# A DLRM tower with three interaction layers: embedding lookups spread otherwise, dense features turned earlier, tile 0 loaded whole, tile 1 loaded from ScalarE's queue

## The chip, the cores and the metric

One core of one Trainium2 chip. The metric is the device time in microseconds (us). Engines: TensorE (PE), VectorE (DVE), ScalarE (ACT), GpSimd (POOL), and SyncE (SP), which in this kernel only issues DMAs.

## The reference, cut to what matters

```
e = stack of 32 table rows per sample                    # 1024 x 32 fields x 16 values, fp32, tables of 1000 to 125000 rows
x0 = h = e                                               # B, F=32, E=16
for W, b in 3 layers:                                    # a compressed interaction network
    z = (x0[:, :, None, :] * h[:, None, :, :])           # B, F*G, E: all products of a field of x0 and a row of h
    y = relu(einsum('oc,bce->boe', W, z) + b)            # 128 rows out
    keep, h = y[:, :64], y[:, 64:]   (last layer: both y)
z = sum over E of all kept rows                          # B x 256
h = concat([z, dense_ctx])                               # B x 272
y = relu(relu(h @ W_top1 + b1) @ W_top2 + b2) @ W_top3   # 512, 256, 1
```

## The kernel before, in words

**Tiles.** The 1024 samples are eight blocks of 128, and a block is four tiles: a tile is four of the 16 embedding values of 128 samples, so it has 512 columns. There are 32 tiles. In the trace a tile takes some 29 to 31 us once the kernel is under way.

**A slot.** The engines work through slots, one per tile. Slot n holds layer 0 of tile n+1, layer 1 of tile n and layer 2 of tile n-1, in an order written out by hand (`SLOT`). An item `(layer, n)` is two chunks of 128 products: VectorE multiplies (`multiply`, L1069), TensorE multiplies the products by the weights (L616). Layer 2 is computed in three passes over split numbers: VectorE writes the product (`unsplit`), ScalarE rounds it (`high`, L828), GpSimd takes the difference (`low`, L499), and TensorE multiplies high by two weights (L624) and then low by one (L639). The last pass of an item stands behind the next item's passes in TensorE's order, and TensorE waits there if GpSimd is not done. Seven of layer 2's eight items go through GpSimd, (2,0) to (2,5) and (2,7); (2,6) is not split. The ring of these buffers has four entries.

**GpSimd's order.** It also issues the lookups: 32 indirect DMAs for each block (`look_up`, L489), one per field, eight per slot, for the block after the current one. Which item they stand behind is a table, `LOOKUPS_AFTER`, with one row for the slot in which a new block's indices are taken (quarter 0) and one for the other three; `LOOKUPS_FIRST` is the number ahead of the first item. In quarter 0 the indices are copied to `ids_now` (L476) by `begin`, behind item (2,2) and the tail (L507), after all lookups of the block before have landed.

**What a tile needs from HBM.** TensorE turns the tile's rows (`turn_x`, L588), ScalarE copies them to `xrows` (`take_x`, L808), SyncE stores them to HBM (`xcols`, L393, 96 KB) and reads them back, once the store has landed, in three layouts: `shifted` (L400, four DMAs of 256 KB) for layer 0, `shifted_tail` (L405, four of 64 KB), and `spread` (L415, four of 1 MB, one per group g of four chunks) for layers 1 and 2. All of them are issued by SyncE in one program order and go to one queue (q1 in the page). The fourth group of a tile is loaded in the next tile's round. Tile 0's `shifted` is not loaded but made by transposes (L671, `FIRST_ORDER`).

**The prologue.** SyncE loads the weights; VectorE and ScalarE reorder them; TensorE turns them in ten groups (`turn`, L560; groups 0 and 1 are layer 0's, 2 to 5 layer 1's, 6 to 9 layer 2's) into two PSUM banks in turn, and VectorE copies each out (L1002; for layer 2 L996, L997 and L1000), so group n waits for the copy of group n-2. Behind all ten TensorE turns the dense features (L576), ScalarE copies them (L784, L786), and VectorE takes their low parts (L1013, L1015). ScalarE's next instruction is the copy of block 0's looked-up rows (`take_rows`, L792), on which GpSimd's `begin` for block 1 and tile 0 depend. GpSimd issues block 0's 32 lookups at once from the start, and behind `begin(1)` another 8 at once; the last three quarters of block 1 follow in the first three slots.

## Time and profile before

| | us |
|---|---|
| median of 3 runs (lowest, highest) | 1094.03 (1093.96, 1094.55) |
| the profiled execution's own time | 1094.61 |
| its span, first to last instruction | 1092.8 |
| PE busy | 1004.2 (92%) |
| DVE busy | 820.0 (75%) |
| POOL busy | 820.0 (75%) |
| ACT busy | 473.9 (43%) |
| DMA, mean of 16 engines | 170 GB/s |

The page's strip of 40 slices has PE at 9 tenths in nearly every slice behind the third, and lower at three places: the first three slices (82 us), slice 13 and slice 29. The granted clock is 8 or 5 tenths in the first slices and drops by a tenth in the same two places later. The rows of timelines further down read: start in us from the span's start, duration in us, engine, line, operation, output<-inputs, shape, count, and in brackets how long the engine was idle before it and what ended that wait.

### The profile page before, as it was taken

To read this page: it belongs to the slowest core of one execution; us is meant where nothing else is said; L and a number is where in the kernel's file an instruction comes from. 1 tells how busy PE (TensorE), PEld (TensorE's weight loads), DVE (VectorE), ACT (ScalarE), POOL (GpSimd) and SP (SyncE) were. 2 spreads that over 40 slices of the span, in tenths; PEclk is the share of its full clock that TensorE was granted. 3 is DMA by queue.
4 is the path that set the end of the run, shared out by engine and by line. 5 is a ranking of instruction groups with operands and counts; after the bars stand their busy time and mean duration, and the time that the engine had idled before them with its cause. 6 is when DMAs were issued, how large, how long until landed. Compare 5 with 4: busy or idle time off the path is not lost.

```text
span 1092.8 us, 11324 instructions
## 1 busy us (share of the span) xinstructions
PE 1004.2 (92%) x3089; PEld 573.0 (52%) x3089; DVE 820.0 (75%) x750; ACT 473.9 (43%) x595; POOL 820.0 (75%) x524
## 2 busy tenths in 40 slices
PE   2168999999989999999999999999899999999988
PEld 2133555555545555555555555555455555555555
DVE  4245787888774887888778877988578877888882
ACT  2132444444443454444535544444335444454453
POOL 6555779797969879797988889797788866666650
PEclk8588999999998999999999999999899999999999
DMA  7079988799985889799987988899787988889200
GB/s 154 5 167 205 208 198 181 166 206 206 193 185 119 187 192 204 158 195 203 201 182 161 201 197 184 171 200 206 155 182 163 198 200 189 189 197 205 75 1 0
DMA packets 49012, 185.45 MB, mean 170 GB/s; under 512 B 17570, under 2 KB 22178, under 8 KB 28388
## 3 DMA queue, kind: packets, MB, share of 16 engines
q1 hardware_dynamic: 40804, 183.15, 75.9%
q0 software_dynamic: 8192, 2.11, 2.1%
q8 instruction: 7, 0.11, 0.1%
q14 instruction: 9, 0.07, 0.0%
HBM read 182.06 MB, written 3.15 MB: 169 GB/s over the span
## 4 chain that ended last, share of the span: by engine, by line
PE 41%; POOL 24%; issue 18%; DVE 8%; ACT 4%; another core or an unknown queue 3%; DMA 2%; SPq 1%; DVEq 0%; POOLq 0%; ACTq 0%
PE y L616 25%; POOL low L499 13%; POOL looked_up L489 9%; PE y L624 9%; PE y L639 5%; DVE unsplit L1069 2%; DVE prod L1069 2%; DVE acc_kept L1100 1%; POOL tail_parts L507 1%; DMA spread<-in_L_rec_W 1%; ACT h L814 1%; PE xT L588 1%; DMA xcols<-xrows 1%; DMA shifted<-xcols 1%
## 5 line engine op out<-in xcount | busy, mean ns | idle before, releaser
L499 POOL TENSOR_TENSOR low<-unsplit,high 128x1024 fp32r<-128x1024 f32 x221 | 530.7, 2411 | 137.3 <-ACT high L828 133.3
L616 PE MATMUL y<-prod,w1T 128*128 128x512 f32 x1024 | 479.3, 596 | 6.1 <-DVE prod L1069 3.3
L1069 DVE TENSOR_TENSOR prod<-spread,h 128x1024 f32<-128x1024 f32 x288 | 346.5, 1213 | 86.5 <-PE y L616 73.5
L828 ACT CAST high<-unsplit 128x1024 fp32r<-128x1024 f32 x224 | 234.1, 1045 | 324.4 <-DVE unsplit L1069 312.8
L1069 DVE TENSOR_TENSOR unsplit<-spread,h 128x1024 f32<-128x1024 f32 x224 | 271.5, 1213 | 102.3 <-ACT h L814 83.8
L489 POOL DMA_INDIRECT looked_up<-in_tbl,ids_now x256 | 246.8, 964 | 75.7 <-issue 71.9
L616 PEld LDWEIGHTS y<-prod,w1T 128*128 128x128 f32 x1024 | 193.1, 191 | 168.0 <-issue 148.4
L624 PE MATMUL y<-high,w2T_high 128*128 128x512 f32 x448 | 227.6, 508 | 1.4 <-ACT high L828 1.4
L639 PE MATMUL y<-low,w2T_high 128*128 128x512 f32 x448 | 203.9, 536 | 22.4 <-POOL low L499 22.1
L624 PE MATMUL y<-high,w2T_low 128*128 128x512 f32 x448 | 178.1, 397 | 0.0
L814 ACT ACTIVATE h<-y,bias 64x512 f32<-64x512 f32 x128 | 83.3, 651 | 165.2 <-PE y L616 156.5
L639 PEld LDWEIGHTS y<-low,w2T_high 128*128 128x128 f32 x448 | 83.1, 191 | 113.0 <-issue 62.7
L616 PE MATMUL y<-prod,w0T 128*128 128x512 f32 x256 | 123.7, 606 | 7.5 <-DVE prod L1069 7.5
L624 PEld LDWEIGHTS y<-high,w2T_high 128*128 128x128 f32 x448 | 85.3, 190 | 47.6 <-issue 28.3
L624 PEld LDWEIGHTS y<-high,w2T_low 128*128 128x128 f32 x448 | 85.1, 190 | 44.0 <-issue 29.5
L1069 DVE TENSOR_TENSOR prod<-shifted,xT 128x1024 f32<-128x1024 f32 x64 | 77.6, 1212 | 25.7 <-DMA shifted<-xcols 20.2
L616 PEld LDWEIGHTS y<-prod,w0T 128*128 128x128 f32 x256 | 49.1, 193 | 51.8 <-issue 47.7
L616 PE MATMUL y<-prod,w2T_whole 128*128 128x512 f32 x128 | 61.9, 607 | 0.0
L1100 DVE TENSOR_TENSOR acc_kept<-acc_kept,kept 128x512 f32<-128x512 f32 x24 | 54.8, 2282 | 0.0
L507 POOL TENSOR_TENSOR tail_parts<-tail,tail_high 128x512 fp32r<-128x512 f32 x32 | 41.0, 1280 | 15.1 <-ACT tail_high L852 15.0
L820 ACT ACTIVATE kept<-y,bias_kept 64x512 f32<-64x512 f32 x64 | 43.7, 682 | 1.6
L808 ACT COPY xrows<-xT 48x512 f32<-48x512 f32 x32 | 18.5, 578 | 44.4 <-PE xT L588 33.2
(115 smaller groups left out, 409.5 us busy)
## 6 DMA issues: line engine op xcount, KB each, us to landing
spread<-xcols SPq DMA_DIRECT2D x128, 1024.0 KB, 9.0
shifted<-xcols SPq DMA_DIRECT2D x124, 256.0 KB
shifted_tail<-xcols SPq DMA_DIRECT2D x124, 64.0 KB
looked_up<-in_tbl,ids_now POOLq DMA_INDIRECT x256
xcols<-xrows SPq DMA_DIRECT2D x32, 96.0 KB
spread<-in_L_rec_W SPq DMA_DIRECT2D x3, 512.0 KB, 6.7
spread<-in_L_rec_W SPq DMA_DIRECT2D x1, 1024.0 KB
wt<-in_W_top SPq DMA_DIRECT2D x2, 512.0 KB, 9.9
```

The costliest lines, as they stand in the source:

```text
L489: pool.indirect_dma_start(out=looked_up[:, f, :], out_offset=None, in_=tables[f][:, :], in_offset=bass.IndirectOffsetOnAxis(ap=ids_now[:, ...
L499: pool.tensor_tensor(low[kind][r][:, :, :], unsplit[kind][r][:, :, :], high[kind][r][:, :, :].bitcast(F32), ALU.subtract).then_inc(s_low[k ...
L507: pool.tensor_tensor(tail_parts[:, :], tail[:, :], tail_high[:, :].bitcast(F32), ALU.subtract).then_inc(s_tail_low, 1)
L616: last = pe.matmul(y[:, :], w, z[:, c, :], start=(n == 0 and c == 0), stop=(item in (LAST0, LAST1) and c == ITEM - 1))
L624: pe.matmul(y[:, :], w[:, ITEM * n + c, :], z[:, c, :], start=(n == 0 and c == 0 and w is w2T_high), stop=False)
L639: last = pe.matmul(accumulator(s, layer)[:, :], w2T_high[:, ITEM * n + c, :], z[:, c, :], start=False, stop=(item == LAST2 and c == ITEM - 1))
L808: act.copy(xrows[:, :], xT[0:XROWS, :]).then_inc(s_xrows, 1)
L814: last = act.activation(h[to, :], y[lanes, :], ACT.Relu, bias=bias[lanes, :])
L820: act.activation(kept[t[1] % 2][lanes, :], y[lanes, :], ACT.Relu, bias=bias_kept[lanes, :]).then_inc(s_kept, 1)
L828: act.copy(high[kind][r][:, :, :], unsplit[kind][r][:, :, :]).then_inc(s_high[kind], 1)
L1069: dve.tensor_tensor(z, x[:, ITEM * n:ITEM * (n + 1), :], b[:, :].unsqueeze(1).to_broadcast([P, ITEM, COLS]), ALU.mult).then_inc(s_made[kin ...
L1100: dve.tensor_tensor(acc_kept[:, :], acc_kept[:, :], z[:, :], ALU.add).then_inc(s_sum_kept, 1)
```

## The change

Four edits. (1) Another table of lookups: in quarter 0 two stand behind (2,2), that is right behind `begin`, none behind (2,3), one behind (2,4), two behind (2,5), three behind (2,7); in the other quarters one ahead of the first item, and one, one, one, two, two behind (2,2), (2,3), (2,4), (2,5), (2,7). (2) TensorE turns the dense features behind layer 1's weights, ahead of layer 2's, and VectorE takes their low parts ahead of its copies of layer 2's weights. (3) Tile 0's four `spread` groups are loaded one after the other. (4) Tile 1's store, its four `shifted` and its four `shifted_tail` loads are issued by ScalarE, right behind its copy of tile 1's rows, with a wait of ScalarE for the store's landing; SyncE waits for the same landing before it issues tile 1's first three `spread` groups.

```diff
--- before.py
+++ after.py
@@ -91,8 +91,8 @@
 
 ADD_KEPT_AFTER = (2, 1)
 FOLD_KEPT_AFTER = (2, 2)
-LOOKUPS_AFTER = ((0, 0, 0, 2, 2, 2, 2), (0, 0, 1, 2, 1, 1, 1))
-LOOKUPS_FIRST = (0, 2)
+LOOKUPS_AFTER = ((0, 0, 2, 0, 1, 2, 3), (0, 0, 1, 1, 1, 2, 2))
+LOOKUPS_FIRST = (0, 1)
 
 
 def kind_of(item, last):
@@ -386,16 +386,13 @@
                            (bias_last[:, :], b2)):
                 sp.dma_start(to, of.rearrange("(p a) -> p a", a=1)).then_inc(s_biases, 16)
 
-            def load_shifted(t):
-
-
+            def store_x(t):
                 sp.wait_ge(s_xrows, number(t) + 1)
                 sp.dma_start(xcols[number(t)], xrows[:, :]).then_inc(s_xcols, 16)
                 sp.wait_ge(s_xcols, 16 * (number(t) + 1))
+
+            def load_shifted(t):
                 x = xcols[number(t)]
-                if isinstance(t[0], int) and number(t) == 0:
-
-                    return
                 for j in range(GROUP):
                     sp.dma_start(shifted[FIELDS * j:FIELDS * (j + 1), :, :],
                                  bass.AP(x.tensor, x.offset + GROUP * j * COLS,
@@ -418,10 +415,9 @@
                              ).then_inc(s_spread[k % 2][g], 16)
 
             def load_factors(t):
+                store_x(t)
                 load_shifted(t)
-
-                if not isinstance(t[0], int) or number(t) >= 1:
-                    load_spread(after(t, -1), GROUPS - 1)
+                load_spread(after(t, -1), GROUPS - 1)
                 for g in range(GROUPS - 1):
                     load_spread(t, g)
 
@@ -436,12 +432,17 @@
             sp.dma_start(bt2[:, :], b_top2.rearrange("(c p) -> p c", p=P), allow_slow_non_contiguous=True).then_inc(s_top_b, 16)
 
             sp.wait_ge(s_stored, PREP_GROUPS)
-            load_factors((0, 0))
+            store_x((0, 0))
+            for g in range(GROUPS):
+                load_spread((0, 0), g)
 
             sp.wait_ge(s_dense_parts, 1)
 
             sp.wait_ge(s_first, len(FIRST_ORDER))
-            load_factors((0, 1))
+
+            sp.wait_ge(s_xcols, 16 * 2)
+            for g in range(GROUPS - 1):
+                load_spread((0, 1), g)
             load_factors((0, 2))
             with sp.Fori(0, BLOCKS - 1) as i:
                 for k in range(START, START + TILES_PER_BLOCK):
@@ -560,22 +561,24 @@
                     last = pe.transpose(prep[n % 2][0:rows, c, :], source(c), ident[:, :])
                 last.then_inc(s_turned, 1)
 
+            def turn_dense():
+                pe.wait_ge(s_dense, 16 * 2 * P // COPY)
+                for b in range(BLOCKS):
+                    last = pe.transpose((y0, y1)[b // GROUP][:, P * (b % GROUP):P * (b % GROUP + 1)], dense_wide[:, b, :],
+                                        ident[:, :])
+                last.then_inc(s_denseT, 1)
+
             pe.wait_ge(s_ident, 1)
             pe.wait_ge(s_sym, 10)
             turn(0, GROUP, P, lambda c: w0_dist[:, P * c:P * (c + 1)])
             turn(1, 1, P, lambda c: w0_dist[:, P * GROUP:P * (GROUP + 1)])
             for g in range(2 * GROUPS):
+                if g == GROUPS:
+                    turn_dense()
                 pe.wait_ge(s_ordered, g // 2 + 1)
                 turn(2 + g, GROUP, P, lambda c: w_turned[g // 2][:, P * (GROUP * (g % 2) + c):P * (GROUP * (g % 2) + c + 1)])
 
             pe.wait_ge(s_stored, PREP_GROUPS)
-
-
-            pe.wait_ge(s_dense, 16 * 2 * P // COPY)
-            for b in range(BLOCKS):
-                last = pe.transpose((y0, y1)[b // GROUP][:, P * (b % GROUP):P * (b % GROUP + 1)], dense_wide[:, b, :],
-                                    ident[:, :])
-            last.then_inc(s_denseT, 1)
 
             def turn_x(t):
 
@@ -790,6 +793,20 @@
                 b = t[0] + t[1] // TILES_PER_BLOCK
                 act.wait_ge(s_looked, 16 * FIELDS * (b + 1))
                 act.copy(emb[:, :, :], looked_up[:, :, :]).then_inc(s_emb, 1)
+
+            def load_second():
+
+                x = xcols[1]
+                act.wait_ge(s_xrows, 2)
+                act.dma_start(x, xrows[:, :]).then_inc(s_xcols, 16)
+                act.wait_ge(s_xcols, 16 * 2)
+                for j in range(GROUP):
+                    act.dma_start(shifted[FIELDS * j:FIELDS * (j + 1), :, :],
+                                  bass.AP(x.tensor, x.offset + GROUP * j * COLS,
+                                          [[COLS, FIELDS], [1, GROUP * COLS]])).then_inc(s_shifted, 16)
+                for j in range(GROUP):
+                    act.dma_start(shifted_tail[FIELDS * j:FIELDS * (j + 1), :],
+                                  x[FIELDS // 2:XROWS, :]).then_inc(s_shifted_tail, 16)
 
             def repeat_fields(t):
 
@@ -871,6 +888,8 @@
                     next_h0(s)
                 if more and x_after is None:
                     take_x(nxt)
+                    if isinstance(s[0], int) and number(nxt) == 1:
+                        load_second()
                 if LAST1 in items:
 
                     act.wait_ge(s_used[WHOLE], plan.entry(s, LAST1) + 1)
@@ -978,7 +997,19 @@
             homes += [w1T[:, GROUP * g:GROUP * (g + 1), :] for g in range(GROUPS)]
             homes += [w2T_high[:, GROUP * g:GROUP * (g + 1), :] for g in range(GROUPS)]
             lows = {2 + GROUPS + g: w2T_low[:, GROUP * g:GROUP * (g + 1), :] for g in range(GROUPS)}
+            def dense_low():
+                dve.wait_ge(s_dense_high, 1)
+                for lanes in (slice(COPY, 2 * COPY), slice(3 * COPY, P)):
+                    for n, bank in enumerate((y0, y1)):
+                        rows = slice(TOP1 * n, TOP1 * (n + 1))
+                        dve.tensor_tensor(dense_parts[lanes, rows], bank[lanes, :], dense_parts[lanes, rows].bitcast(F32),
+                                          ALU.subtract)
+                dve.tensor_tensor(wt_dense_parts[HALF:P, :], wt_dense[HALF:P, :], wt_dense_parts[HALF:P, :].bitcast(F32),
+                                  ALU.subtract).then_inc(s_dense_parts, 1)
+
             for n, home in enumerate(homes):
+                if n == 2 + GROUPS:
+                    dense_low()
                 dve.wait_ge(s_turned, n + 1)
                 source = prep[1][:, 0, :] if n == 1 else prep[n % 2]
                 if n == 1:
@@ -1006,14 +1037,6 @@
             dve.wait_ge(s_neg, 2)
             dve.wait_ge(s_stored, PREP_GROUPS)
 
-            dve.wait_ge(s_dense_high, 1)
-            for lanes in (slice(COPY, 2 * COPY), slice(3 * COPY, P)):
-                for n, bank in enumerate((y0, y1)):
-                    rows = slice(TOP1 * n, TOP1 * (n + 1))
-                    dve.tensor_tensor(dense_parts[lanes, rows], bank[lanes, :], dense_parts[lanes, rows].bitcast(F32),
-                                      ALU.subtract)
-            dve.tensor_tensor(wt_dense_parts[HALF:P, :], wt_dense[HALF:P, :], wt_dense_parts[HALF:P, :].bitcast(F32),
-                              ALU.subtract).then_inc(s_dense_parts, 1)
 
             dve.sem_inc(s_sum2, 1)
             dve.sem_inc(s_z, 1)
```

## Rows read from the trace of the kernel before

**Rows 1.** Waits of TensorE, 130 to 1000 us: us in total, times, longest.
```profile
PE y L639 <- POOL low L499: 20.3, 19, 6.7
```

**Rows 2.** Timeline of TensorE: the turns of a tile's rows, one per slot.
```profile
308.44 0.60 PE L588 MATMUL xT<-ident,four_times 128*128 128x128 f32 x4
346.95 0.60 PE L588 MATMUL xT<-ident,four_times 128*128 128x128 f32 x4
...
646.25 0.60 PE L588 MATMUL xT<-ident,four_times 128*128 128x128 f32 x4
676.92 0.60 PE L588 MATMUL xT<-ident,four_times 128*128 128x128 f32 x4
707.76 0.60 PE L588 MATMUL xT<-ident,four_times 128*128 128x128 f32 x4
737.31 0.60 PE L588 MATMUL xT<-ident,four_times 128*128 128x128 f32 x4
766.63 0.60 PE L588 MATMUL xT<-ident,four_times 128*128 128x128 f32 x4
803.07 0.60 PE L588 MATMUL xT<-ident,four_times 128*128 128x128 f32 x4
```

**Rows 3.** Timeline of GpSimd, behind a copy of indices.
```profile
53.92 0.97 POOL L489 DMA_INDIRECT looked_up<-in_tbl,ids_now  x1 [0.81 <-POOL ids_now L476]
...
517.53 0.20 POOL L476 COPY ids_now<-ids_sb 128x32 int32 x1
...
532.31 2.39 POOL L499 TENSOR_TENSOR low<-unsplit,high 128x1024 fp32r<-128x1024 f32 x1
...
539.58 7.06 POOL L499 TENSOR_TENSOR low<-unsplit,high 128x1024 fp32r<-128x1024 f32 x3
```

**Rows 4.** Timeline of TensorE and of GpSimd, waits in two slots of one block.
```profile
542.02 0.73 PE L639 MATMUL y<-low,w2T_high 128*128 128x512 f32 x2 [0.46 <-POOL low L499]
...
576.64 2.39 POOL L499 TENSOR_TENSOR low<-unsplit,high 128x1024 fp32r<-128x1024 f32 x1 [5.11 <-ACT high L828]
```

**Rows 5.** Timeline of GpSimd, the two long pauses between lookups.
```profile
326.85 0.95 POOL L489 DMA_INDIRECT looked_up<-in_tbl,ids_now  x1 [9.36 <-issue]
...
762.54 0.94 POOL L489 DMA_INDIRECT looked_up<-in_tbl,ids_now  x1 [0.30 <-issue]
...
771.35 0.96 POOL L489 DMA_INDIRECT looked_up<-in_tbl,ids_now  x1 [5.45 <-issue]
```

**Rows 6.** Timeline of the prologue.
```profile
40.06 0.42 DVE L996 COPY w2T_whole<-y 128x256 f32<-128x256 f32 x1 [6.98 <-remote]
...
44.79 0.94 POOL L489 DMA_INDIRECT looked_up<-in_tbl,ids_now  x1 [0.30 <-issue]
...
50.66 1.07 ACT L784 CAST dense_parts<-y 128x512 fp32r<-128x512 f32 x2 [31.47 <-remote]
...
52.14 0.63 ACT L792 COPY emb<-looked_up 128x512 f32<-128x512 f32 x1
```

**Rows 7.** Timeline of tiles 1 and 2, first slots.
```profile
70.32 0.34 SPq L393 DMA_DIRECT2D xcols<-xrows  x1
...
76.39 1.73 SPq L400 DMA_DIRECT2D shifted<-xcols  x4
...
83.15 1.22 DVE L1069 TENSOR_TENSOR prod<-shifted,xT 128x1024 f32<-128x1024 f32 x1 [6.94 <-DMA shifted<-xcols]
...
85.14 0.62 ACT L851 CAST tail<-tail 64x512 fp32r<-64x512 f32 x1 [13.93 <-DVE tail L1051]
...
99.03 5.40 PE L616 MATMUL y<-prod,w1T 128*128 128x512 f32 x8 [2.71 <-issue]
...
112.57 3.27 PE L616 MATMUL y<-prod,w0T 128*128 128x512 f32 x4 [1.92 <-DVE prod L1069]
```

**Rows 8.** Busy time by stretch: A:B, length, busy us per engine (instructions), clock, DMA share, GB/s.
```profile
66.00:74.00 8.00, 5.68 (x17) 2.55 (x17) 4.62 (x4) 3.43 (x5) 6.17 (x7) 1.00 1.03 213
74.00:78.00 4.00, 4.00 (x11) 1.85 (x10) 1.22 (x1) 0.00 (x0) 1.00 (x2) 1.00 0.28 61
```

## The prediction, made before the changed kernel was run

> **What bounds the kernel now.** I read the page's strip of slices first: TensorE is busy nearly throughout, so only the places where it is not can give anything. They are the start, slice 13, slice 29, and, too short for the strip, a wait per slot here and there. The waits of TensorE over the steady part come next: nearly all of them are the low pass waiting for GpSimd, 20.3 us in 19 waits, the longest 6.7 [rows 1]. The turn of a tile's rows stands once in each slot, so its spacing measures a slot [rows 2]. A block read there has slots of 30.67, 30.84, 29.55 and 29.32 us. The last has no wait, so a block loses some 1.37 + 1.52 + 0.23 = 3.1 us, and the first two parts belong to the slots behind the copy of indices. Two slots are far longer: 38.51 (308.44 to 346.95) and 36.44 (766.63 to 803.07), 7.67 and 5.77 more than their like in the block shown. GpSimd's timeline has their cause: between two lookups it stands 9.36 us, and 5.45 us with a low pass in between [rows 5]. These are lookups 113 and 226 counted from 0, twice the same distance. So I take them for something that fills up by count, whatever the order is. Last I read the start in the timelines.
>
> **Lookups, the usual block.** Lookups in a run cost GpSimd 1.22 us each: low (2,7) ends at 532.31 + 2.39 = 534.70, and four lookups later the next slot's (2,0) begins at 539.58 [rows 3]. The table changes what stands ahead of each low. Counted from `begin`, there are now 2, 2, 3, 5 lookups ahead of (2,3), (2,4), (2,5), (2,7), where there were 0, 2, 4, 6, and 9 instead of 10 ahead of the next slot's (2,0). The price is that a lookup now reads the indices straight behind their copy: it began 0.81 us after such a copy [rows 3], where low (2,3) follows in 0.24 (517.73 to 517.97). Worked through: copy ends 517.73, first lookup 518.54, second ends 520.75, (2,3) to 523.1, (2,4) to 525.5, one lookup, (2,5) to 529.05, two lookups, (2,7) from 531.45 to 533.85, four lookups, (2,0) ends 541.1. It ended at 541.97, just ahead of the pass that TensorE began at 542.02 [rows 4]. Of that slot's 1.37 us of waits, TensorE, which would else be there at 542.02 - 1.37 = 540.65, keeps 0.5: **0.9 us gained**, bounds 0 (a first lookup 0.9 dearer would eat it) and 1.4 (no wait left). The second slot's 1.52 us I leave: the low (2,2) at 576.64 began when ScalarE was ready, after GpSimd had been idle 5.11 us [rows 4], so no lookup is in its way. The 0.23 of the third slot I leave as well: from (2,2) on, five lookups stand ahead of (2,7), as before. Five of the six steady blocks: 5 x 0.9 = 4.5 us, bounds 0 and 7.
>
> **The first pause.** Lookup 113 is the second of its quarter. It stood right behind lookup 112, ahead of (2,0). It now stands behind (2,2) and the tail. In between come three lows of 2.4, one idle stretch and the tail's 1.3, over 10 us, longer than the 9.36 us pause [rows 5]. If the pause is a wait for earlier lookups to land, it is over by then: **7.7 us gained**. Bounds: 0 if it is work of its own that GpSimd does wherever it falls, 9.2 (38.51 - 29.32) with every wait gone.
>
> **The second pause.** Lookup 226 is the third of quarter 0. Lookup 225 ended at 762.54 + 0.94 = 763.48, 226 began at 771.35, so GpSimd was free to go on 7.87 us after it [rows 5]. Now 224 and 225 stand behind `begin`, then (2,3) and (2,4), 4.8 us, and a gap of 0.16, then 226: it still waits 2.9 us. GpSimd brings (2,0) at 541.1 + 2.9 = 544.0 in the clock of the block above, 3.35 us behind TensorE's free run, where the slot lost 36.44 - 29.32 = 7.12: **3.8 us gained**, bounds 0 and 7.1. Steady part: 4.5 + 7.7 + 3.8 = 16.0 us.
>
> **The prologue.** ScalarE stood from 19.2 until 50.66 for the turned dense features, then copied block 0's rows at 52.14, though their last lookup had been issued at 44.79 [rows 6]. With the dense turns first, that copy, GpSimd's `begin(1)` and its eight lookups come up to 5 us earlier (landing at 47, my estimate from 44.79 + 0.94 and 1 to 2 us of flight). But TensorE turns tile 0 only when layer 2's weights are copied. Those copies ended near 41.8 (40.06 and three copies), and the eight dense turns behind them were done only at 50.6, 8.8 us, though four turns of a tile's rows take 0.6 [rows 2]. These turns are now ahead of layer 2's, and the copies behind VectorE's 3.3 us of dense parts. So the copies end between 43 (the turns hide) and 53 (they cost what they did), and tile 0's turn, 53.9 before, comes between 48.8 and 53.3. I take 51, **3 us earlier**, the middle, because no row says why these turns end so late.
>
> **Tile 0's four loads and tile 1's from ScalarE.** Before, tile 1's store was issued at 70.32 behind tile 0's three `spread` loads in the same queue and its readers at 76.39, 6.1 us later; the DMA engines meanwhile ran dry, 61 GB/s in 74 to 78 after 213 in the stretch before [rows 7, 8], a hole worth (1 - 61/213) x 4 = 2.9 us. VectorE stood 6.94 us for `shifted` until 83.15. Now the fourth `spread` group fills the hole, and the store goes to another queue. The trace has no queue of ScalarE's. Bounds for the store's flight: nothing, and the 6.1 with a fourth load ahead of it, 1 MB at 213 GB/s, 11 in all. Of the 6.1, some 3.7 went by while the engines were still full [rows 8], so 2.4 are its own; I take 3.5 with the other queue's packets in between, and half the engines for the readers while SP's loads run beside them. ScalarE's copy of tile 1's rows is 3 to 4.5 us earlier, near 65.5; readers issued at 69.3; their first 1 MB at 105 GB/s takes 10 us; VectorE starts on tile 1's layer 0 near 80.3, **2.9 us earlier**. ScalarE's nine issues (0.42 us each, SP's four took 1.73) and its wait, some 8 us, lie in its idle 13.93 us ahead of 85.14 [rows 7]; without that cover they would delay everything one for one. What is late next is layer 1 of tile 1: its slot began at 99.03 and now at 96.1. TensorE ran 11.6 us from there and stood 1.92 until 112.57 for the product with tile 2's `shifted` [rows 7]. These bytes come behind the same total but without the hole and from an earlier start, 5.9 us sooner, so this wait is gone: 2.9 + 2 = 4.9 us, and 1.1 for less time at the lower clock (8 or 5 tenths in the strip's first slices, to which idle stretches led). **Start-up 6 us**, bounds 2.7 and 11.
>
> The Trainium skill, "DMA: Bandwidth & Descriptors", section "Issuing engines are not separate DMA queues", speaks against this edit: issuing from several engines saves only the sequencer's time. Its section "Queues, rings and completion order" speaks for it: SP and ACT own a row of rings each, served in turns of a packet. No row of this trace has both queues busy. By the first the store would come no sooner than it was (third rival below), by the second it passes the loads.
>
> **Sum.** 16.0 + 6 = 22.0 off the profiled execution's 1094.6 gives 1072.6; the median is 0.6 below that execution, so **1072.0 us**.
>
> **Rivals.** (a) The pauses are work and not waiting: both stay, the second still in a place without slack. For it, that 9.36 and 5.45 differ by more than the low pass between; against it, 9.36 and 7.87 counted from the lookup before are near each other. Gains 0.9 x 6 + 6 = 11.4: 1082.6. (b) TensorE's late turns are no work of its own and hide: tile 0 starts 5 us earlier and the lower clock goes: start-up 10 to 11, 1067. For it, 8.8 us for eight turns; against it, layer 2's groups are just as late one after another. (c) ScalarE's store comes no sooner than in the shared queue: `shifted` is there at 83 as before, and only tile 2's wait and the hole remain, 2.7 us: 1075.3. (d) Slower: the lookups behind `begin` pause in every block, since they are now the first to need the copied indices and directly follow the landing wait of `begin`. A pause of p delays (2,0), where GpSimd is already last, by p in six blocks. It decides from 22/6 = 3.7 us on; at rows 5's 9.36 it is 1072 + 56 = 1128. Against it: 256 lookups show two such pauses, and the gap behind a copy was 0.81 [rows 3, 5]. (e) The waits only move, to VectorE's ring of four and to DMA: no change. Against it, slots without lookups run at 29.3 in this same trace.
>
> **Chances.** Forecast 0.45, (a) 0.15, (b) 0.16, (c) 0.16, (d) 0.03, (e) 0.02; 0.03 for less than half of everything, still faster. A difference of 0.2%, 2.2 us, is what a measurement here can tell from none. Faster 0.95, same 0.02, slower 0.03. The range takes in (b), (c) and most of (a): 1064 to 1083.
>
> **What would show it.** In the changed trace: slots of 29.8, 30.8, 29.5, 29.3; no gap near 9 us ahead of lookup 113 and one near 3 ahead of 226; TensorE's waits for low near 10 us in all; tile 0's turn at 48.8 to 53.3; the first `shifted` of tile 1 issued by ACT 3 to 4 us behind its store, no stretch below 150 GB/s between 58 and 100; TensorE's layer 1 of tile 1 in its slot of layer 2 near 96, no wait near 108. I am wrong in the mechanism if the pause ahead of 113 stays, or if VectorE gets tile 1's `shifted` no earlier than tile 0's shift alone would give; wrong in size if the first slot of a block still takes 30.5.

## The result, and the profile after

The changed kernel takes 1096.49 us (median of 10 runs) against 1093.99 us for the kernel before beside it: ratio 1.0019, 95% interval 1.0010 to 1.0028. It is 2.5 us slower where 22 us less were forecast. One run of the changed kernel (1204.41 us) and one of the kernel before (2676.57 us) lay far outside; the medians are hardly moved by them. The profiled execution took 1094.6 us with a span of 1092.7 us, 0.1 us less than before.

The table did its part. The waits of TensorE between 130 and 1000 us answer [rows 1]; the turns of a tile's rows answer [rows 2].

```profile
PE y L642 <- POOL low L500: 8.9, 15, 0.8
PE y L619 <- DVE prod L1092: 2.1, 7, 0.6
```
```profile
652.93 0.60 PE L591 MATMUL xT<-ident,four_times 128*128 128x128 f32 x4
682.94 0.60 PE L591 MATMUL xT<-ident,four_times 128*128 128x128 f32 x4
713.78 0.60 PE L591 MATMUL xT<-ident,four_times 128*128 128x128 f32 x4
743.35 0.60 PE L591 MATMUL xT<-ident,four_times 128*128 128x128 f32 x4
```

The wait for the low pass is 8.9 us instead of 20.3, its longest 0.8 instead of 6.7, and a slot with the copy of indices is 30.01 us instead of 30.67. GpSimd's timeline answers [rows 3, 5]: the first lookup behind a copy, then lookup 113 (347.77) and lookup 226 (772.50).

```profile
524.85 0.21 POOL L477 COPY ids_now<-ids_sb 128x32 int32 x1
525.88 0.99 POOL L490 DMA_INDIRECT looked_up<-in_tbl,ids_now  x1 [0.82 <-POOL ids_now L477]
...
347.77 0.97 POOL L490 DMA_INDIRECT looked_up<-in_tbl,ids_now  x1 [0.30 <-issue]
...
766.64 0.94 POOL L490 DMA_INDIRECT looked_up<-in_tbl,ids_now  x1 [0.30 <-issue]
767.60 4.74 POOL L500 TENSOR_TENSOR low<-unsplit,high 128x1024 fp32r<-128x1024 f32 x2
772.50 0.96 POOL L490 DMA_INDIRECT looked_up<-in_tbl,ids_now  x1 [0.16 <-issue]
```

Both pauses are gone. Between ScalarE's copy of the fifth tile's rows and that of the last one lie 807.5 us (173.52 to 981.01); before there were 825.0 (156.04 to 980.99). So in these two profiled executions 17.5 us were gained after 174 us, and since the spans are equal, as much was lost ahead of it. The timeline of ScalarE and VectorE at the start answers [rows 6, 7]:

```profile
25.29 1.07 ACT L787 CAST dense_parts<-y 128x512 fp32r<-128x512 f32 x2 [5.81 <-remote]
...
47.41 0.62 ACT L795 COPY emb<-looked_up 128x512 f32<-128x512 f32 x1 [20.52 <-DMA looked_up<-in_tbl,ids_now]
48.06 1.05 ACT L817 COPY four_times<-emb 128x512 f32<-128x512 f32 x1
56.12 0.58 ACT L825 COPY xrows<-xT 48x512 f32<-48x512 f32 x1 [7.01 <-remote]
...
72.78 0.40 ACTq L801 DMA_DIRECT2D xcols<-xrows  x1
81.96 1.97 ACTq L804 DMA_DIRECT2D shifted<-xcols  x4
83.95 2.02 ACTq L808 DMA_DIRECT2D shifted_tail<-xcols  x4
...
97.53 1.22 DVE L1092 TENSOR_TENSOR prod<-shifted,xT 128x1024 f32<-128x1024 f32 x1 [20.17 <-DMA shifted<-xcols]
104.92 0.69 DVE L1074 TENSOR_TENSOR tail<-shifted_tail,xT 128x512 f32<-128x512 f32 x1 [6.17 <-DMA shifted_tail<-xcols]
```

TensorE begins tile 1's layer 0 right behind VectorE's first product; the kernel before, then the changed one:

```profile
84.52 3.75 PE L616 MATMUL y<-prod,w0T 128*128 128x512 f32 x4 [5.24 <-DVE prod L1069]
```
```profile
98.89 3.52 PE L619 MATMUL y<-prod,w0T 128*128 128x512 f32 x4 [17.09 <-DVE prod L1092]
```

Four distances matter here. The dense features and the looked-up rows are there early, as planned, but tile 0's rows are copied at 56.12 us (55.07 before). Tile 1's store takes 9.2 us from issue to the instruction behind it (6.1 before). Its readers take 15.6 us from issue to VectorE's first product (6.8 before), and the tail 7.4 us more. Then the DMA engines, which were to have no hole, have a far longer one than [rows 8] showed; the columns are those:

```profile
78.00:84.00 6.00, 3.80 (x9) 1.33 (x7) 0.00 (x0) 0.00 (x0) 0.00 (x0) 1.00 0.50 121
84.00:90.00 6.00, 0.00 (x0) 0.00 (x0) 0.00 (x0) 1.05 (x1) 0.00 (x0) 0.58 1.01 203
90.00:98.00 8.00, 0.00 (x0) 0.00 (x0) 0.47 (x1) 0.00 (x0) 0.00 (x0) 0.50 1.03 207
98.00:104.00 6.00, 3.52 (x4) 1.17 (x4) 0.75 (x1) 0.00 (x0) 0.00 (x0) 0.66 0.95 205
104.00:110.00 6.00, 3.21 (x5) 1.51 (x5) 5.08 (x5) 1.23 (x2) 2.59 (x3) 0.62 0.00 0
110.00:116.00 6.00, 6.00 (x13) 2.69 (x12) 1.32 (x3) 1.99 (x3) 4.47 (x6) 0.81 0.09 7
116.00:122.00 6.00, 3.29 (x11) 1.56 (x11) 3.88 (x5) 3.60 (x5) 3.07 (x4) 1.00 0.34 72
```

Tile 2's rows can be turned only in tile 1's slot, which waits for those tails. SP stores them at 117.93 us (96.95 before). Until then it issues nothing, since all that it still has to load, tile 1's fourth `spread` group too, stands behind that store in its program. TensorE begins tile 2's layer 0 at 129.76 us, 17.2 later than in [rows 7].

### The profile page after: what moved, and what is told of

Its sections match the earlier page's. It is cut to its first block, busy times and chain, and to the rows that moved or that the text cites. A ratio compares the mean times of both kernels' runs of the same rounds, so it can differ in the third digit from the quotient of the medians.

```text
span 1092.7 us, 11323 instructions
## 1 busy us (share of the span) xinstructions
PE 999.4 (91%) x3089; PEld 571.0 (52%) x3089; DVE 823.2 (75%) x750; ACT 474.0 (43%) x595; POOL 820.7 (75%) x524
## 4 chain that ended last, share of the span: by engine, by line
PE 40%; POOL 27%; issue 16%; DVE 8%; ACT 3%; DMA 3%; another core or an unknown queue 1%; ACTq 0%; DVEq 0%; POOLq 0%
PE y L619 25%; POOL low L500 16%; POOL looked_up L490 11%; PE y L627 8%; PE y L642 5%; DVE prod L1092 3%; DVE unsplit L1092 2%; DMA shifted_tail<-xcols 2%; DMA xcols<-xrows 1%; DVE acc_kept L1123 1%; ACT h L831 1%; POOL tail_parts L508 1%; PE xT L591 1%; DVE low L1100 0%
## 5 line engine op out<-in xcount | busy, mean ns | idle before, releaser
L619 PE MATMUL y<-prod,w0T 128*128 128x512 f32 x256 | 124.3, 609 | 23.9 <-DVE prod L1092 23.9
L1123 DVE TENSOR_TENSOR acc_kept<-acc_kept,kept 128x512 f32<-128x512 f32 x24 | 60.8, 2533 | 0.0
L817 ACT COPY four_times<-emb 128x512 f32<-128x512 f32 x32 | 34.9, 1092 | 14.1 <-issue 13.3
```

What stands on the lines that cost most here:

```text
L619: last = pe.matmul(y[:, :], w, z[:, c, :], start=(n == 0 and c == 0), stop=(item in (LAST0, LAST1) and c == ITEM - 1))
L817: act.copy(four_times[:, :, :, :], emb[:, :, QUAD * q:QUAD * (q + 1)].rearrange("p f e -> p e f").unsqueeze(2).to_broadcast([P, QUAD, GROU ...
L1123: dve.tensor_tensor(acc_kept[:, :], acc_kept[:, :], z[:, :], ALU.add).then_inc(s_sum_kept, 1)
```

## The experiments

The kernel before took 1089.8 us on the chip of the first four runs and 1094.0 to 1095.0 us on the two chips of the others. That is more than noise (the executions on one chip spread over 2 to 3 us), and what goes with it, shown further down, bears on the dense turn. So ratios are compared across chips and times only within one.

### The halves apart (chip of 1089.8 us)

Table alone: the kernel before with two lines changed.

```diff
-LOOKUPS_AFTER = ((0, 0, 0, 2, 2, 2, 2), (0, 0, 1, 2, 1, 1, 1))
-LOOKUPS_FIRST = (0, 2)
+LOOKUPS_AFTER = ((0, 0, 2, 0, 1, 2, 3), (0, 0, 1, 1, 1, 2, 2))
+LOOKUPS_FIRST = (0, 1)
```


> The kernel before with the new table of lookups alone. Theory T (the table is worth what the steady slots of the changed kernel show, 825.0 - 807.4 = 17.6 us between the same two copies of rows, and the whole loss sits in the start): about 1077 us. Rival S (the steady slots only look shorter because the late start left the buffers full): 1085 to 1094 us.

Measured 1074.39 us, ratio 0.9857 (0.9841 to 0.9874): 15.4 us less.

Start alone: the changed kernel with the old table (the diff above, reversed).

> The changed kernel with the old table of lookups: only the three edits of the start. Theory T: the start costs 18 us, so 1112 us, with slots of 30.7, 30.8, 29.5, 29.3 and both pauses of GpSimd back. Rival S: 1096 to 1103 us.

Measured 1103.27 us, ratio 1.0126 (1.0109 to 1.0142): 13.5 us more. Both pauses are back, 9.36 us and 5.14 us. The store went out at 64.92 us, the readers at 75.56, and VectorE had them at 91.16. The time is at the edge of the rival's range, but the run before has ruled out what the rival stands on, a table that gives nothing. So the loss is the start's own and does not need the new table. I had put it at 18 us, from the result. Of these, 2.0 are the table's, by a slot that it lengthens (below), and the rest of the difference fits the price of the dense turn, which shows only on other chips.

### Which part of the new order of transfers costs (same chip)

All from SP: the changed kernel, but tile 1's store and readers are SP's again, behind tile 0's four loads and ahead of tile 1's.

```diff
-            sp.wait_ge(s_xcols, 16 * 2)
+            store_x((0, 1))
+            load_shifted((0, 1))
             for g in range(GROUPS - 1):
                 load_spread((0, 1), g)
...
-                        load_second()
```


> The changed kernel, but tile 1's store and readers go back to SyncE, behind tile 0's four loads and ahead of tile 1's spread loads. Theory T (a transfer is served behind everything issued before it, on whatever queue, and transfers issued together from both queues share the engines): the store lands no later than from ScalarE, near 82 us, the shifted rows then have the engines alone and land near 89 instead of 97.7, the tails near 90.5 instead of 105: 1080 us. Rival R (queues are served in turns, so ScalarE's queue did help the store): the store lands later than 82.2, and the kernel is as slow as the changed one, 1096 us, or slower.

Measured 1074.81 us, ratio 0.9862 (0.9846 to 0.9878).

SP holds back: ScalarE issues as in the changed kernel, and SP waits with tile 1's loads.

```diff
             sp.wait_ge(s_xcols, 16 * 2)
+            sp.wait_ge(s_shifted, 16 * GROUP)
+            sp.wait_ge(s_shifted_tail, 16 * GROUP)
```


> The changed kernel, but SyncE issues tile 1's spread loads only when tile 1's shifted rows and tails have landed; ScalarE still issues store and readers. Theory T (sharing costs the readers 9 to 15 us, the queue of ScalarE nothing by itself): shifted near 89, 1081 us, within 2 us of the run with everything on SyncE. Rival Q (ScalarE's queue is slow by itself): shifted still 14 us or more behind the store, 1090 us or more.

Measured 1076.38 us, ratio 0.9872 (0.9855 to 0.9888). The timelines of SP in the first and of ScalarE in the second of these two runs:

```profile
66.68 0.34 SPq L391 DMA_DIRECT2D xcols<-xrows  x1
76.36 1.72 SPq L397 DMA_DIRECT2D shifted<-xcols  x4
...
83.07 1.22 DVE L1077 TENSOR_TENSOR prod<-shifted,xT 128x1024 f32<-128x1024 f32 x1 [11.28 <-DMA shifted<-xcols]
```
```profile
67.47 0.40 ACTq L803 DMA_DIRECT2D xcols<-xrows  x1
77.03 1.75 ACTq L806 DMA_DIRECT2D shifted<-xcols  x4
...
83.83 1.22 DVE L1094 TENSOR_TENSOR prod<-shifted,xT 128x1024 f32<-128x1024 f32 x1 [11.77 <-DMA shifted<-xcols]
```

The store's flight is 9.7 us from SP's queue and 9.6 us from ScalarE's: another queue gained nothing. In both, the fourth load of 1 MB landed at 75.8 and 76.7 us, just ahead of the store. And with nothing issued beside them the readers take 6.7 and 6.8 us, from either queue, instead of the 15.6 of the changed kernel. I had expected 1080 and 1081 us; the surplus over the table alone is only 0.4 and 2.0 us, so the fourth load ahead of the store is nearly free, and nearly the whole price lies in SP's three loads of 1 MB issued in the same microsecond as ScalarE's readers: the second of these runs changes nothing else.

### The same on a chip with late turns

In the four runs so far a result of TensorE's turns in the prologue reaches the engine that waits for it some 1.2 us after the turn's start (quick turns). In the two profiles of the result, and on the chips from here on, many reach it several us later (late turns). First the changed kernel itself, for the chip's sake; there is no edit.

> The changed kernel itself, so that its own number stands beside the others'. My theory: the table gives 15 to 17 us wherever it runs; the order of the transfers at the start takes 13.5 back (the run with the start alone), and where TensorE's turns of the weights are quick there is nothing to win by turning the dense features earlier. So 1.5 to 3 us faster than the kernel before if the turns are quick in its prologue (layer 2's copies done before 34 us), and 1 to 3 us slower, as in the result, if they are late (copies done near 51). The rival, that the two halves of the change disturb each other, expects the result's 2.5 us slower in either prologue.

Measured 1096.54 us, ratio 1.0028 (1.0014 to 1.0041); layer 2's copies ended at 56.7 us, the late kind.

Table and dense turn: the changed kernel with SP's part and the loads as before.

```diff
-            store_x((0, 0))
-            for g in range(GROUPS):
-                load_spread((0, 0), g)
+            load_factors((0, 0))
...
-            sp.wait_ge(s_xcols, 16 * 2)
-            for g in range(GROUPS - 1):
-                load_spread((0, 1), g)
+            load_factors((0, 1))
...
-                        load_second()
```


> The kernel before with the new table and the dense features turned ahead of layer 2's weights; the loads and stores as before. My theory: with quick turns tile 0's rows wait for the last lookup to land, so this is the time of the run with the table alone, ratio 0.9857, within 0.1% (tile 0's rows copied at 50 to 51 us). The prediction's theory, that the dense turn brings tile 0 some 3 us forward: ratio 0.983. If the turns are late, tile 0's rows come at 56 as in the changed kernel, and the ratio is up to 0.2% worse.

Measured 1085.01 us, ratio 0.9902 (0.9882 to 0.9923): worse than I allowed for. Tile 0's rows were copied at 61.75 us. Its four executions lie between 1082.27 and 1088.53 us, and the profiled one is the slowest of them.

Three loads ahead of the store, from ScalarE:

```diff
             store_x((0, 0))
-            for g in range(GROUPS):
+            for g in range(GROUPS - 1):
                 load_spread((0, 0), g)
...
             sp.wait_ge(s_xcols, 16 * 2)
+            sp.wait_ge(s_shifted, 16 * GROUP)
+            load_spread((0, 0), GROUPS - 1)
```


> The changed kernel, ScalarE still issuing tile 1's store and its readers, but SP holds back tile 0's fourth load and all of tile 1's until the shifted rows have landed, so only three loads stand ahead of the store. My theory (a transfer is served behind what was issued before it, whichever queue it is in): the store lands near 72, the readers near 79, TensorE begins tile 1 near 80, and the time is that of the table alone plus about 1 us for the gap in the DMA engines, ratio 0.986 to 0.988. The rival, that issuing from ScalarE costs by itself (its copies and its own work are held up): the ratio stays at 0.99 or more, with the readers landed but TensorE's first product of tile 1 later than 82.

Measured 1087.35 us, ratio 0.9931 (0.9914 to 0.9947), above the range given. The transfers did as expected: from tile 0's copy of rows (63.71) to the readers on VectorE (91.56) it took 27.9 us, in the run before this one 28.3 us (61.75 to 90.02). It was tile 0 that was late, 13 us later than I took for granted. Up to there its prologue is that of the changed kernel, whose rows came at 56.12 and 57.87, so one trace tells little of how late a prologue is. The rival, a price of ScalarE's issues, is out, since VectorE had the rows as early as with SP's.

Store ahead of the third load, on the table alone:

```diff
-            load_factors((0, 0))
+            load_shifted((0, 0))
+            load_spread((0, 0), 0)
+            load_spread((0, 0), 1)
...
-            load_factors((0, 1))
+            sp.wait_ge(s_xrows, 2)
+            sp.dma_start(xcols[1], xrows[:, :]).then_inc(s_xcols, 16)
+            load_spread((0, 0), 2)
+            sp.wait_ge(s_xcols, 16 * 2)
+            load_readers((0, 1))
+            load_spread((0, 0), GROUPS - 1)
...
```


> The kernel before with the new table, all DMAs from SP, but tile 1's store issued behind two of tile 0's loads, the third between the store and the wait for it. My theory: the store lands near 69.5 instead of 72, but its readers stand behind the third load, which now comes 2 to 4 us later, so shifted lands at 78 to 79 and the time is that of the table alone within 0.1%: the bytes ahead of tile 1's layer 0 are what counts and not the queue they are in. If the time from the rows to the readers were a round trip independent of the bytes in flight, shifted would land near 76.5 and the ratio be 0.2% better.

Measured 1078.95 us, ratio 0.9861 (0.9844 to 0.9877), the table's. The store took 2.0 us instead of 6.1, and the readers, now behind the third load, were with VectorE no earlier (83.80 us; 83.15 in the kernel before). What counts is the bytes issued ahead of the readers.

### Why the turns are late (a third chip, 1094.3 us)

Filler: eight transposes more behind each of layer 2's turns, on the table alone.

```diff
+                if g >= GROUPS:
+                    for c in range(8):
+                        pe.transpose(h1[:, P * (c % 4):P * (c % 4 + 1)], ident[:, :], ident[:, :])
```


> The kernel before with the new table, and eight more transposes of the identity into a PSUM bank not yet in use behind each of layer 2's four turns, which compute nothing that is used. The question is why, in some profiles (the kernel before and the changed one among them), what TensorE signals between 20 and 60 us arrives 5 to 15 us after its instruction. If the signals are late because TensorE is nearly idle there, they are quick with it kept busy: layer 2's copies done by 33 us and tile 0's rows at 51 (kernel before, late: 41 and 55). If each transposition is itself slow there, the eight more make it later still, tile 0's rows after 58. If it comes from elsewhere, nothing moves by more than 2 us. Where the turns are quick anyway, the time is that of the table alone within 0.1%, ratio 0.986, and this says nothing.

Measured 1084.24 us, ratio 0.9909 (0.9890 to 0.9929); tile 0's rows at 60.14 us. More work makes it later, which speaks against idleness as the reason. It does not rule it out: the filler is 1 us of work per turn, and TensorE stood 16 us behind one of them. The next run decides more.

Lookups held, on the table alone:

```diff
             next_ids(0)
+            pool.wait_ge(s_stored, PREP_GROUPS)
             for f in range(FIELDS):
```


> The kernel before with the new table, and GpSimd's first 32 lookups held until all weights are turned and copied. If the late signals of TensorE come from GpSimd's lookups running beside them, all four of layer 2's copies are done by 26 us, the lookups end 40 us later, and the time is about 20 us worse (some 1095 to 1100) from the later start of tile 0 alone. If they come from elsewhere, the copies are as late as without the hold (39 to 42) where they are late at all, and the time is 30 us worse or more.

Measured 1092.89 us in one run. Below, TensorE's timeline in this run, then in one of the same chip whose prologue is the same but for the hold (the three quarters of the table alone, below); the turns of layer 2's last two groups of weights in each.

```profile
19.73 0.63 PE L561 MATMUL y<-ident,prod 128*128 128x128 f32 x4 [1.12 <-DVE w2T_low L1001]
21.05 0.63 PE L561 MATMUL y<-ident,prod 128*128 128x128 f32 x4 [0.69 <-DVE w2T_low L1001]
```
```profile
22.91 1.08 PE L560 MATMUL y<-ident,prod 128*128 128x128 f32 x4 [2.49 <-DVE w2T_low L1000]
27.20 1.09 PE L560 MATMUL y<-ident,prod 128*128 128x128 f32 x4 [3.21 <-DVE w2T_low L1000]
```

A step of turn and copies is 1.3 us with the lookups held and 4.3 us with them; the last copy ended at 23.9 us instead of 42.2, since the copies behind these two turns were later still. Nothing else differs up to there but the lookups. On the chip of 1089.8 us the steps were 1.3 us with the lookups running. So as far as one trace of each kernel tells, it takes both, the lookups and the chip.

Then I split the table. Only the quarter with the copy of indices, and only the other three, each on the kernel before:

```diff
-LOOKUPS_AFTER = ((0, 0, 0, 2, 2, 2, 2), (0, 0, 1, 2, 1, 1, 1))
+LOOKUPS_AFTER = ((0, 0, 2, 0, 1, 2, 3), (0, 0, 1, 2, 1, 1, 1))
```


> The kernel before with the new order only in the quarter of each block that holds the copy of indices. My theory: that slot shrinks from 30.7 to 30.0 us in each block, the pause ahead of lookup 226 goes (slot of 36.0 to 36.4 becomes 30.0), and the pause of 9.36 us ahead of lookup 113, which is in another quarter, stays with its slot of 37.8 to 38.5: in all 10 of the 16 us less, 1084 or 0.990 to 0.992. If a pause is set by how many lookups GpSimd has issued back to back anywhere, lookup 113's changes as well.

```diff
-LOOKUPS_AFTER = ((0, 0, 0, 2, 2, 2, 2), (0, 0, 1, 2, 1, 1, 1))
-LOOKUPS_FIRST = (0, 2)
+LOOKUPS_AFTER = ((0, 0, 0, 2, 2, 2, 2), (0, 0, 1, 1, 1, 2, 2))
+LOOKUPS_FIRST = (0, 1)
```


> The kernel before with the new order only in the three quarters without the copy of indices. My theory: only the pause ahead of lookup 113 goes, its slot 30.8 again, 7 to 7.7 us less; the slots with the copy stay at 30.7 and the one with lookup 226 at 36.0 to 36.4: ratio 0.993 to 0.994. The two halves then add up to the table's 15 to 16.5 us.

Measured 1095.89 us and 1082.29 us in one run each, beside 1094.27 for the kernel before. GpSimd's timeline, lookups 113 and 226 in the first of these, then 226 in the second:

```profile
331.77 0.95 POOL L489 DMA_INDIRECT looked_up<-in_tbl,ids_now  x1 [9.36 <-issue]
...
772.53 0.96 POOL L489 DMA_INDIRECT looked_up<-in_tbl,ids_now  x1 [0.16 <-issue]
```
```profile
760.04 0.96 POOL L489 DMA_INDIRECT looked_up<-in_tbl,ids_now  x1 [5.40 <-issue]
```

Each half removes the pause that lies in it. But I had put the gain of the usual block into the wrong half: the first run has slots of 31.26 us with the copy, worse than 30.67, the second 29.9. The prediction's own chain says why: `LOOKUPS_FIRST` sets how many lookups stand ahead of the next slot's (2,0), 10 in the first run with 0.82 us of wait on top, 9 in the second without it. The second ran at 0.989, better than expected, and the two don't add up to the whole (12.0 less and 1.6 more against 14.8 less), since each keeps or makes a wait that the other takes away.

### The sum on one chip (1095.0 us)

Table and transfers without the dense turn: the changed kernel with `turn_dense` back behind layer 2's turns.

```diff
-                if g == GROUPS:
-                    turn_dense()
...
             pe.wait_ge(s_stored, PREP_GROUPS)
+
+
+            pe.wait_ge(s_dense, 16 * 2 * P // COPY)
+            for b in range(BLOCKS):
...
-                if n == 2 + GROUPS:
-                    dense_low()
...
             dve.wait_ge(s_stored, PREP_GROUPS)
-
+            dense_low()
```


> The changed kernel with the dense features turned behind layer 2's weights again: the new table and the new order of the start's transfers. My theory so far: the order of the transfers costs 11 to 13.5 us by itself (13.5 in the run with the start alone where turns were quick, 11.5 between the changed kernel and the one without the new transfers where they were late), so table and transfers give about 2 to 4 us less than the kernel before: ratio 0.996 to 0.999, with tile 1's shifted rows 15 us behind their issue. Where the turns are late, it is 5 to 6 us faster than the changed kernel of the same call, which is the dense turn's price; where they are quick, the two are within 1 us. The rival, that the dense turn costs only together with the new transfers, expects this kernel at the changed one's time less 10 us or more.

Table and dense turn, the second lookups held:

```diff
+            pool.wait_ge(s_xT, 1)
             begin(1)
```


> Table and early dense turn, with the transfers as before, and GpSimd's second block of lookups held until tile 0's rows are turned. The run with all lookups held had every turn of TensorE within 1 us of its instruction, though layer 2's last came at 50 us in its neighbours. So if it is lookups beside a turn that make it late, tile 0's turn, issued near 57 (late turns), is there 1.2 us later, its rows are copied by 58 to 59 instead of 61.75, and the time is 3 to 4 us below the run without this hold: ratio 0.986 to 0.988 instead of 0.9902. If the held lookups mattered by something else than what runs beside the turn, tile 0's rows stay at 61 to 62. Where turns are quick anyway, tile 0's rows come at 50 to 51 and the time is the table's, ratio 0.986.

The table alone and the changed kernel, once more, without an edit:

> The kernel before with the new table alone, once more, as the base for the dense turn's price on this chip: ratio 0.986 on either kind of prologue, since the table works in the steady part only; tile 0's rows copied at 55 where turns are late, at 50.6 where they are quick.

> The changed kernel beside its parts on one chip. If the parts add up: table 0.986, dense turn 5 to 6 us (late turns) or nothing (quick turns), transfers 11 to 13.5 us; so 1.5 to 3.5 us slower than the kernel before where the turns are late, and about 2 us faster where they are quick.

| on one chip | us | ratio to before (95%) |
|---|---|---|
| before | 1095.02 | |
| table | 1080.25 | 0.9871 (0.9855 to 0.9888) |
| table, transfers | 1093.25 | 0.9985 (0.9975 to 0.9994) |
| table, transfers, dense turn (the change) | 1097.14 | 1.0018 (1.0009 to 1.0028) |
| table, dense turn, second lookups held | 1079.18 | 0.9855 (0.9839 to 0.9871) |

The table takes off 14.8 us, the transfers put 13.0 back, the dense turn 3.9: 2.1 us slower in all. The dense turn costs without the transfers too: 0.9902 (in the earlier runs on this chip) against 0.9871, some 3.4 us with an uncertainty of about 3. The rival, that it costs only together with them, had asked for 10 us here and is out. With the second lookups held its cost is gone: 1079.18 us is the table's time.

What makes tile 0's turn late? TensorE and ScalarE in the changed kernel of this chip, then with the second lookups held (and the transfers as before, which begin only behind this turn):

```profile
54.75 1.11 PE L591 MATMUL xT<-ident,four_times 128*128 128x128 f32 x4 [15.29 <-issue]
...
60.63 0.58 ACT L825 COPY xrows<-xT 48x512 f32<-48x512 f32 x1 [10.57 <-remote]
```
```profile
53.87 1.11 PE L591 MATMUL xT<-ident,four_times 128*128 128x128 f32 x4 [10.29 <-DVE w2T_low L1015]
...
55.02 0.58 ACT L811 COPY xrows<-xT 48x512 f32<-48x512 f32 x1 [6.07 <-PE xT L591]
```

The same four transposes reach ScalarE 5.9 us after their start amid lookups and 1.15 us with the lookups held. The kernel that differs from the second by the hold alone, table and dense turn, has 5.2 us (56.53 to 61.75), and the result's changed kernel 3.8 (52.30 to 56.12). With the hold the rows came even before the 58 to 59 us expected, since layer 2's last copy ended sooner too, at 53.8 us instead of 56.5. Layer 2's last step, 6.0 to 9.5 us amid lookups on these two chips, was 1.65 us in the two traces where it fell after the first block's lookups and ahead of the second's (the held one, 51.47 to 53.12, and the filler's, 51.25 to 52.90). But lookups beside a turn do not always delay it. The changed kernel's first run on this chip has lookups from 49.28 to 59.14 and is quick:

```profile
56.72 1.12 PE L591 MATMUL xT<-ident,four_times 128*128 128x128 f32 x4 [14.66 <-issue]
...
58.05 1.09 POOL L490 DMA_INDIRECT looked_up<-in_tbl,ids_now  x1 [0.30 <-issue]
...
57.87 0.58 ACT L825 COPY xrows<-xT 48x512 f32<-48x512 f32 x1 [8.66 <-issue]
```

So every late turn found here had lookups beside it or shortly ahead of it, the holds took the delay away, and yet one turn amid lookups was on time. That they take part is shown; what else it takes is not.

## Why the prediction was wrong, step by step

**Usual block, 0.9 us each.** Right in kind, 0.7 in size (30.67 to 30.01), and by the step that it named, one lookup fewer ahead of the next slot's (2,0).

**First pause, 7.7 us.** Right in the number: the slot of 38.51 us became 30.8. That the pause is a wait for earlier lookups fits this, and no run shows it.

**Second pause, 3.8 us.** Too low: no 2.9 us pause was left ahead of lookup 226. It began 5.86 us after lookup 225, where it had begun 8.81 after it before, so a pause that ends at a fixed time after the lookup ahead of it isn't what this is. With it the steady part gave 17.5 us of trace for the 16.0 forecast. That count begins one slot late: the slot ahead of it, from 126 us on in the kernel before, is 32.0 us with the table instead of 30.0, and TensorE waits 2.4 us for low there instead of 0.3. The table alone gained 14.8 and 15.4 us, so the forecast of 16.0 was about right, with two errors that cancel.

**Prologue, tile 0's turn 3 us earlier.** Wrong in what counts. The turn itself was issued at 52.30 us, inside the range given and 1.6 us earlier than before, but its rows reached ScalarE 3.8 us later instead of 1.15, so they were copied 1.05 us later than before, and 2 to 8 us later on the chip of the sum (57.87, 60.63, 61.75 and 63.71 in four kernels with the early dense turn, 55.74 with the table alone). Turn and copy of tile 0's rows in the kernel before, then from the changed one its dense turn:

```profile
53.92 1.12 PE L588 MATMUL xT<-ident,four_times 128*128 128x128 f32 x4 [10.08 <-ACT four_times L800]
...
55.07 0.58 ACT L808 COPY xrows<-xT 48x512 f32<-48x512 f32 x1 [1.21 <-PE xT L588]
```
```profile
21.18 1.97 PE L567 MATMUL y<-ident,spread 128*128 128x128 f32 x8 [2.90 <-DMA spread<-in_W_top]
```

I had taken late turns as a given of the place and put the copies' end between 43 and 53 us; it was 52.2, and 56.7 elsewhere. Two things were put at nothing. The early dense turn has to wait 2.9 us for its own load, and with the turn's work that starts layer 2's turns at 22.95 us instead of 18.20 and their first low part at 30.98 instead of 22.52, 8.5 us deeper into the stretch with lookups. Their steps there, 4.3, 5.6 and 8.7 us in the kernel before, were 5.5, 7.0 and 8.1 in the changed one and 7.7, 10.5 and 6.7 with table and dense turn alone. And the early copy of block 0's rows brought `begin(1)` forward, so that its eight lookups ran beside tile 0's turn. [Rows 6] had shown an engine free at 45.7 and eight turns of 8.8 us; I weighed that GpSimd's end bounded `emb`, and not that GpSimd was what ran beside the slow turns. On the chip with quick turns the lookups' landing bounds tile 0 anyway (rows copied at 50.65 us by the table alone, 50.15 with the dense turn), so the step has nothing to win there either. Rival (b), late turns that hide, fell with it.

**Tile 1's transfers, 6 us of start-up with the term before.** This is the step that failed by its size: 13 us lost. It had two terms. I took 3.5 us for the store's flight, between bounds of 0 and 11, and it was 9.2: rival (c). Its first packet moved at 79.15 us, 6.4 us after issue, when the last packet of the four loads had just started (79.05). The Trainium skill says in "DMA: Bandwidth & Descriptors", section "Issuing engines are not separate DMA queues", that issuing from several engines saves only the sequencer's time; the trace agrees, with 9.7 and 9.6 us from the two queues. For the loads issued *later*, the Trainium skill's section "Queues, rings and completion order" on the same page has each DMA engine take a packet from each queue in turn; the trace agrees in kind, as the readers shared the engines with SP's three loads. But I priced that sharing as an even one, 10 us for the first 1 MB, and stopped there. Between 83 and 96 us SP's queue moved 1.72 MB and ScalarE's 1.03: the readers had some 37% of the engines and not half. Measured were 15.6 us to the first product, and the tails, last in ScalarE's queue, came at 104.9 behind nearly all of SP's loads. Rival (c) priced at 1075 only the store's part. That order is what costs: the bytes that tile 1 needs first end last; TensorE enters tile 1 at 98.89 us (84.52 before); tile 2's rows, turned in tile 1's slot, are 21 us later; and the wait that I had called gone became a hole of 12 us in the DMA engines. Held back, the same loads cost 2.0 us, so of the 13 some 11 are the price of issuing them beside the readers. The 1.1 us that the term counts for the clock shows in no run: executions of the changed kernel with a mean granted clock of 0.966 to 0.986 took 1093.3 to 1097.7 us in no order.

**Sum and chances.** 22 forecast, 2.5 the other way: in the profiled execution 17.5 in the steady part where 16.0 stood, and 17.5 lost at the start (2.0 of them the table's slot above) where 6 should have been gained; the medians differ by 2.5. The slower case that I wrote down was a pause behind `begin`; 0.82 us, as in [rows 3], refuted it. No slower case stood on the transfers, though it was the one part of the change in which a shared resource already ran at 213 GB/s with work on the critical path on both sides.

**What stays open.** Why turns amid lookups are late on two of these chips, though not every one, and not on the one of 1089.8 us; why the steps grow between 20 and 50 us; and what the pauses of 113 lookups wait for. The changed kernel was not timed on the chip with quick turns: the table's 15.4 less and the start's 13.5 more suggest 1088 us, 2 us faster, but that is a sum and no measurement.

The versions without the new transfers beat both kernels: the table alone at 0.9857 and 0.9871, with the dense turn and the second lookups held at 0.9855. These three can't be told apart.

## What to carry to other kernels

Here, with the DMA engines full, the time of a transfer that the critical path waited for was set by the bytes issued ahead of it and beside it, in whatever queue. Before issuing bulk loads earlier or from another engine, list what becomes late, down to the last small transfer, and whose next transfer waits on that. A step moved forward also moves what it triggers: ask what will now run beside it. And try parts of a change alone, since 15 us won and 17 us lost looked from outside like a change that does nothing.

## What the hardware showed unexpectedly

On two chips of three, results of TensorE's turns amid GpSimd's indirect lookups reached their reader late in a nearly idle prologue: tile 0's turn in three traces 3.8 to 5.9 us after its start, and the turn issued at 27.61 us in the kernel before after 12.5 us (40.06). With the lookups held or over it took 1.15 us, but so it did once amid them. On the third chip it was 1.1 to 1.2 us in all four traces, and layer 2's steps were 1.3 us amid lookups. In the changed kernel's trace the signals of five groups of turns, issued from 53.65 to 58 us at 0.85 us each, came 0.06 us apart between 61.8 and 62.0 us. The plain timings fit: 1089.8 us against 1094 to 1095 for one kernel, where tile 0's rows with the table alone come at 50.65 us against 55.74. In the steady part, with eight lookups in a slot and not 32 in a row, no such delay shows (behind the first block, slots of 29.3 to 30.9 us with the table on all chips, but for two slots of one trace). The granted clock does not explain it: the late steps ran at 1.00 (2.4 GHz) in the changed kernel between 30 and 58 us and the quick ones at 0.50 (1.2 GHz) with the table alone between 22 and 50.
